# Attention and experts on one core: bias of the exponential on GpSimd, the second score half one unit later, the product with the values seven units behind

## What is computed

```python
q = (x @ Wq + bq).reshape(1, B * N, H, hd)          # x: layernorm of the input, 2048 rows
q = _fq_sym(q * scale, axis=-1)                     # s = max|q| / 127, at least 1e-8; round(q / s) * s
k = _fq_sym(k, axis=-1)
v = _fq_sym(v, axis=2)
attn = jax.nn.softmax(jnp.einsum('bhqd,bhkd->bhqk', q, k), axis=-1)
attn = _fq_unsigned(attn, axis=-1)                  # s = max / 255; round(attn / s) * s
out = jnp.einsum('bhqk,bhkd->bhqd', attn, v)
x = x + out @ Wp + bp
```

## Time and profile before

| | |
|---|---|
| median of 3 runs | 1599.62 us (1597.22 to 1603.06) |
| profiled execution | 1606.57 us, span of the trace 1604.8 us |
| TensorE, VectorE, ScalarE, GpSimd busy over the span | 83%, 65%, 53%, 53% |
| L540, 256 times | 311.9 us busy, 1218 ns each |
| L570, 256 times | 328.2 us busy, 1282 ns each |
| L493, 256 times | 536.3 us busy, 2095 ns each |
| L488, 256 times | 97.9 us busy, 382 ns each |
| L625, 256 times | 485.4 us busy, 1901 ns each |

### The profile page before, as it was taken

One profiled execution on the slowest core, in us unless ns is written; L12 is line 12 of the kernel. 1 busy time (PEld: TensorE's weight loads), 2 busy tenths in 40 slices (PEclk: granted clock), 3 DMA queues, 4 the chain that ended last, 5 costly groups with the idle time before them and its releaser, 6 DMA issues.

```text
span 1604.8 us, 28516 instructions
## 1 busy us (share of the span) xinstructions
PE 1335.0 (83%) x7922; PEld 664.3 (41%) x7923; DVE 1036.9 (65%) x1863; ACT 851.7 (53%) x1183; POOL 855.4 (53%) x772
## 2 busy tenths in 40 slices
PE   7997787778778777887877659889988998989996
PEld 3443333344344444443443334444444444444443
DVE  6456789999999999999999827623323233332331
ACT  2223699888899888898998931112211111111221
POOL 1001477677777777777776710535444444444451
PEclk9999689898898899889898969999999999999999
DMA  7332466665666556566666647276767656666455
GB/s 225 86 72 59 73 119 125 112 119 113 129 136 130 120 118 121 118 127 131 131 115 111 115 166 250 84 229 161 198 181 213 189 129 190 162 192 129 88 93 165
DMA packets 383109, 221.56 MB, mean 138 GB/s; under 512 B 344801, under 2 KB 344929, under 8 KB 378786
## 3 DMA queue, kind: packets, MB, share of 16 engines
q1 hardware_dynamic: 365186, 177.36, 45.4%
q0 software_dynamic: 17872, 43.58, 14.3%
HBM read 103.42 MB, written 36.70 MB: 87 GB/s over the span
## 4 chain that ended last, share of the span: by engine, by line
DVE 26%; PE 25%; issue 22%; DMA 19%; ACT 4%; POOL 2%; DVEq 1%; POOLq 0%; SPq 0%; ACTq 0%
DMA acc_dram<-mem 16%; DVE mem L540 15%; PE psS L750 10%; PE psS L758 4%; DVE mem L570 3%; PE psS L434 3%; PE psAV L405 2%; PE psS L1559 2%; DMA mem<-xn_dram,mem 1%; ACT mem L493 1%; PE psT L1187 1%; PE psP L1540 1%; DMA mem<-xn_dram 1%; DVE mem L516 1%; PE psP L742 1%
## 5 line engine op out<-in xcount | busy, mean ns | idle before, releaser
L625 POOL TENSOR_SCALAR mem<-mem 128x2048 bf16<-128x2048 uint8 x256 | 485.4, 1901 | 183.6 <-DMA mem<-mem 161.5
L493 ACT ACTIVATE mem<-mem 128x2048 uint8<-128x2048 f32 x256 | 536.3, 2095 | 12.4
L434 PE MATMUL psS<-mem 128*128 128x512 bf16 x1024 | 351.6, 430 | 158.4 <-DVE mem L570 114.5
L750 PE MATMUL psS<-mem 128*128 (+1 forms) x752 | 358.4, 620 | 0.0
L570 DVE TENSOR_SCALAR_CACHE_REDUCE mem<-psS,mem 128x1024 f32<-128x1024 f32 x256 | 328.2, 1282 | 23.9
L540 DVE TENSOR_SCALAR_CACHE_REDUCE mem<-psS 128x1024 f32<-128x1024 f32 x256 | 311.9, 1218 | 18.6 <-PE psS L434 18.5
L778 ACT ACTIVATE mem<-mem 128x256 f32<-128x256 f32 x94 | 39.3, 418 | 368.2 <-DVE mem L784 368.2
L1157 POOL DMA_INDIRECT acc_dram<-mem x78 | 125.4, 1607 | 195.5 <-DVE mem L1257 152.3
L784 DVE TENSOR_SCALAR mem<-psS 128x512 f32<-128x512 f32 x94 | 65.0, 692 | 220.9 <-PE psS L750 219.4
L434 PEld LDWEIGHTS psS<-mem 128*128 128x128 bf16 x1024 | 74.2, 103 | 317.2 <-DVE mem L540 146.9
L750 PEld LDWEIGHTS psS<-mem 128*128 128x128 f32 x752 | 141.6, 199 | 149.5 <-issue 147.4
(11 more groups left out here) (207 smaller groups left out, 1253.8 us busy)
## 6 DMA issues: line engine op xcount, KB each, us to landing
mem<-in_moe_w SPq DMA_DIRECT2D x33, 1536.0 KB, 9.4
mem<-in_x SPq DMA_DIRECT2D x32, 256.0 KB, 2.9
acc_dram<-mem SPq DMA_DIRECT2D x29, 256.0 KB, 2.3
mem<-mem SPq DMA_TRANSPOSE x288, 3.1
xn_dram<-mem SPq DMA_DIRECT2D x17, 256.0 KB, 2.1
mem<-in_ctx_in SPq DMA_DIRECT2D x16, 256.0 KB, 3.2
mem<-xn_dram SPq DMA_DIRECT2D x16, 256.0 KB, 4.4
mem<-acc_dram SPq DMA_DIRECT2D x16, 256.0 KB, 4.3
```

The source lines that it names most:

```text
L434: last = nc.tensor.matmul(psS[c][:, k * D:(k + 1) * D], qT[p][:, h, :], kT[:, h, c * HALF + k * D:c * HALF + (k + 1) * D], start=True, sto ...
L493: nc.scalar.activation(p8[slot], S[slot], ACT.Exp, bias=NB[:, slot:slot + 1], scale=sq[p][:, h:h + 1], accum_out=Z[p][:, h:h + 1]).then_in ...
L625: nc.gpsimd.tensor_scalar(pb[slot], pT[slot].bitcast(U8).rearrange("p (j q b) -> p j b q", b=2, q=P), 1.0, 0.0, ALU.mult, ALU.add).then_in ...
L750: last = nc.tensor.matmul(bankG[o], xT[o if xo is None else xo][:, c, :], w(c * 2 * I, 2 * I), start=(c == 0), stop=(c == DC - 1))
```

## The change

- VectorE's second half is reduced one step later: in step n it takes half 0 of unit n and half 1 of unit n-1. TensorE makes the halves in the same order.
- The bias moves from ScalarE (L488) to GpSimd, at the head of its step n. It waits for the second half of unit n there. The tile of ln 255 goes, since the value is an immediate now.
- LAG becomes 7 and BEHIND 3. The output stages stand at 9, 10, 12, 14, routing at 11 and 13, the copy of the logits at 14, the division at LAG = 7 as before, and the eviction of the transposed attention on ScalarE at h = 7.
- The query scale takes its lower bound from a tile `least` of 1e-8 instead of an immediate, as scalar_tensor_tensor; the product with QSCALE (L520) goes into the rounding instruction.
- GpSimd spreads the queries three times instead of four; the fourth part is zeroed once ahead of the loop.

```diff
-    LAG = 6
-    BEHIND = 2
-    OUT_AT = (9, 11, 13, 14)
+    LAG = 7
+    BEHIND = 3
+    OUT_AT = (9, 10, 12, 14)
...
             if there(t):
                 if h == 0:
                     pe.wait_ge(queries_moved[p], 16 * (tt + 1))
-                scores(0)
+                scores(0, n, p, h)
...
-            if there(t):
-                scores(1)
+            if within(n - 1):
+                scores(1, n - 1, p if h else 1 - p, (h - 1) % H)
...
-            if h == 10:
+            if h == 11:
                 pe_route(pe, t - 2, 0)
-            if h == 12:
+            if h == 13:
                 pe_route(pe, t - 2, 1)
...
-            if h == 8 and there(t - 1):
+            if h == 7 and there(t - 1):
                 if due(t):
                     act.wait_ge(attn_tr, t)
...
-                if h == 0:
-                    act.wait_ge(minus_ready, t + 1)
-                act.wait_ge(half_max[1], n + 1)
-                nc.scalar.activation(NB[:, slot:slot + 1], M[:, 2 * slot + 1:2 * slot + 2], ACT.Identity,
-                                         bias=ln255[:], scale=nsq[p][:, h:h + 1]).then_inc(bias_ready, 1)
                 act.wait_ge(bias_ready, n + 1)
...
-            nc.vector.tensor_scalar(sq[p], amax, QSCALE / 127.0, 1e-8, ALU.mult, ALU.max).then_inc(q_scale, 1)
+            nc.vector.scalar_tensor_tensor(sq[p], amax, QSCALE / 127.0, least, ALU.mult, ALU.max).then_inc(q_scale, 1)
             dve.wait_ge(q_scale, t + 1)
             nc.vector.reciprocal(rc, sq[p]).then_inc(q_recip, 1)
-            dve.wait_ge(q_recip, t + 1)
-            nc.vector.tensor_scalar(rz2, rc, QSCALE, None, ALU.mult).then_inc(q_factor, 1)
...
-            nc.vector.tensor_tensor(hv(q8), hv(psP[:]), bc(rz2, HD), ALU.mult).then_inc(q8_ready, 1)
+            nc.vector.scalar_tensor_tensor(hv(q8), hv(psP[:]), QSCALE, bc(rc, HD), ALU.mult, ALU.mult).then_inc(q8_ready, 1)
...
-            if h == LAG + 1 and there(t - 1):
+            if h == LAG and there(t - 1):
...
-            if there(t):
-                dve.wait_ge(scores_made[1], n + 1)
-                dve.wait_ge(half_max[0], n + 1)
-                nc.vector.tensor_scalar(S[slot][:, HALF:TK], psS[1][:], 1.0, M[:, 2 * slot:2 * slot + 1],
-                                            ALU.mult, ALU.max, accum_out=M[:, 2 * slot + 1:2 * slot + 2]).then_inc(half_max[1], 1)
-            if h == 13 and there(t - 2):
+            if within(n - 1):
+                dve.wait_ge(scores_made[1], n)
+                dve.wait_ge(half_max[0], n)
+                nc.vector.tensor_scalar(S[before][:, HALF:TK], psS[1][:], 1.0, M[:, 2 * before:2 * before + 1],
+                                            ALU.mult, ALU.max,
+                                            accum_out=M[:, 2 * before + 1:2 * before + 2]).then_inc(half_max[1], 1)
+            if h == 14 and there(t - 2):
...
-            nc.gpsimd.tensor_scalar(qst, hv(q8).unsqueeze(2).to_broadcast([P, H, 4, HD]),
+            nc.gpsimd.tensor_scalar(qst[:, :, 0:3, :], hv(q8).unsqueeze(2).to_broadcast([P, H, 3, HD]),
                                         1.0, 0.0, ALU.mult, ALU.add).then_inc(q_spread, 1)
...
+            if there(t):
+                slot = l % NS
+                if h == 0:
+                    pool.wait_ge(minus_ready, t + 1)
+                    apart(pool, t + 1)
+                pool.wait_ge(half_max[1], n + 1)
+                apart(pool, n + 1)
+                if due(n - NS + 1):
+                    pool.wait_ge(exp_done, n - NS + 1)
+                    apart(pool, n - NS + 1)
+                nc.gpsimd.tensor_scalar(NB[:, slot:slot + 1], M[:, 2 * slot + 1:2 * slot + 2],
+                                            nsq[p][:, h:h + 1], LN255, ALU.mult, ALU.add).then_inc(bias_ready, 1)
             if not isinstance(n, int) or 0 <= n - BEHIND < TT * H:
...
+            nc.gpsimd.memset(least, 1e-8).then_inc(least_ready, 1)
+            nc.gpsimd.memset(qst[:, :, 3, :], 0.0).then_inc(least_ready, 1)
```

More of the change, by code:

```diff
@@ L249, in attention_and_experts @@
         q_amax = sem("q_amax")
-        q_factor = sem("q_factor")
+        least_ready = sem("least_ready")
         q_recip = sem("q_recip")
@@ L349, in there, with within @@
             return not isinstance(t, int) or 0 <= t < TT
+        def within(n):
+            return not isinstance(n, int) or 0 <= n < TT * H
         block = es.enter_context(nc.Block())
@@ L428, in pe_step, with scores @@
             t = 2 * tt + p
-            def scores(c):
-                if due(n):
-                    pe.wait_ge(half_max[c], n)
+            def scores(c, m, pm, hm):
+                if due(m):
+                    pe.wait_ge(half_max[c], m)
                 for k in range(HALF // D):
-                    last = nc.tensor.matmul(psS[c][:, k * D:(k + 1) * D], qT[p][:, h, :],
-                                            kT[:, h, c * HALF + k * D:c * HALF + (k + 1) * D],
+                    last = nc.tensor.matmul(psS[c][:, k * D:(k + 1) * D], qT[pm][:, hm, :],
+                                            kT[:, hm, c * HALF + k * D:c * HALF + (k + 1) * D],
                                             start=True, stop=True)
@@ L534, in dve_step @@
             t = 2 * tt + p
-            slot = l % NS
+            slot, before = l % NS, (l - 1) % NS
             if there(t):
@@ L1383, in _ @@
                 nc.gpsimd.tensor_scalar(vTb[:, m, :], vT8[:, m, :], 1.0, 0.0, ALU.mult, ALU.add).then_inc(v_whole, 1)
+            pool.wait_ge(least_ready, 2)
             pool_spread(pool, 0, 0)
@@ L1507, in _ @@
                 nc.vector.tensor_scalar(vT8[:, m, :], vT[:, m, :], rv[:, m:m + 1], None, ALU.mult).then_inc(v8_ready, 1)
+            dve.wait_ge(least_ready, 1)
             dve_scale(dve, 0, 0)
```

8 lines of the change are left out of this document (2 added, 6 removed).

## The result

The changed kernel takes 1639.94 us (median of 4 runs, 1632.57 to 1646.98) against 1600.76 (1597.22 to 1603.06) for the kernel before on the same chip: 1.024 times, with a 95% interval of 1.0196 to 1.0284. It was forecast at 1592, 0.5% faster; it is 2.4% slower, and outside the range of 1567 to 1619. The profiled execution took 1641.72 us with a span of 1640.0, against a span of 1604.8 before.

The account below looks back on a forecast made before the run. VectorE, busy 95 of 100 us, was taken to bound the attention loop. A gross gain of 46.5 us less 39 us for late queries and TensorE's clock gave 7.5 us faster, 1592 on the median's scale, range 1567 to 1619.

Parts of the forecast that it names:

- The swap's gain: VectorE's two reductions per unit: 0.21 us saved in 11 of 16 units, plus 0.12, so 2.43 us a tile.
- Gross gain: VectorE in the attention loop: 16 x 2.43 from the swap plus 15 x 0.51 from the query scale, 46.5 us.
- The fourth rival: VectorE's halves: the 0.21 us does not go away, being the pipeline's end and not the semaphore; 1612 us, chance 0.09.
- The third rival: Query scale on VectorE: L516's new form does not wait for GpSimd, 10 us more gained, 1582 us; chance 0.09.
- The late queries: Tile boundary: the next tile's query transpose lands late and VectorE stalls 1.7 us at each of 15 boundaries.
- freeing it is worth nothing: ScalarE: it loses the 0.38 us of L488 but has slack already, so no gain was counted.
- All nothing: Moved eviction, output stages and routing, the values' seven-unit lag, and the memsets: no effect on the time.
- The clock: TensorE's lower granted clock: 0.25 us a tile at output matmuls, 0.65 behind the boundary wait, at 15 boundaries.
- Rival 2: TensorE's low clock lasts from the boundary into the projections, 1.7 us a tile beyond the forecast; 1618 us, chance 0.24.
- a backlog falls only 0.2 a unit: GpSimd's queue: bias and conversion take 2.15 us against VectorE's 2.36 a unit, so it fits but catches up slowly.
- The last sentence: Sign of error: if VectorE waits for exponentials rather than queries, GpSimd's backlog was sized too low.
- GpSimd 90% busy: Sign that the forecast is right: GpSimd 90% busy with little wait for DMA.

Follow-up runs that it names:

- the fastest kernel: The changed kernel with the bias back on ScalarE and the query transpose sent at h = 10 instead of 11: 1574.4 us.

## Why the prediction was wrong, point by point

**The swap's gain: right.** 1.15 us between the halves, as taken from the neighbour at h = 15. Gross gain 41.5 us measured against 46.5; of the 5 us missing, L513's longer wait is 15 x 0.16 = 2.5. The swap alone shortens VectorE's work by 37.7 us, 2.4 of them at L513, for 16 x 2.43 = 38.9. The fourth rival is out, and with it the rule of the Trainium skill as it was weighed there (VectorE: DVE Perf Modes, "The DRAIN you can't avoid"): starts moved closer by 0.21 us when the dependence on the instruction just in front went. The third rival is out too, by the 983 ns.

**The late queries: the right mechanism, sized too low.** The forecast had the issue at step 13 + 5.6, and the quoted tile has 498.55 to 504.02, 5.5. It had landing after 4.5: so it is. It had 9.1 from step 13 to step 0: 498.55 to 507.64, when L581 ends, is 9.1. It had 1.7 of stall, and the tile has 1.98, the difference being a first pair of matmuls at a lower clock (1.07 us from the first's start to VectorE's, for 0.7). Over all boundaries it is 38.9 / 15 = 2.6. The transposes are issued 5.8 us behind step 13 in the mean (5.4 to 6.1) for 5.6, because the bias of h = 11 starts at +1.7 in the mean and not at +1.3; VectorE begins 5.8 behind the issue for 5.2 (5.6 to 5.8, and 7.1 at the first boundary); and at the first and last boundary its own way is shorter. There was no stall at the boundaries before, so this costs 38.9 us more, where the forecast had 15 x 1.7 = 25.5: 13 us short.

**ScalarE and what stands in its queue: the step that failed.** The forecast has "freeing it is worth nothing" for ScalarE, and "All nothing" for the eviction and the stages that the change moves. I priced what ScalarE saved and not what stands in its queue. The copy of the next tile's input (L478) keeps its place at h = 2, and it is in no term of the sum. When the exponentials come late, so does this copy behind the one of h = 1, and TensorE's projections wait for it at h = 4. That costs 28.0 - 3.3 = 24.7 us at h = 5, and the edit that moves the copy takes that stall away. With half of the conversion left out it is 14.8 instead of 28.0, and with the halves not swapped 3.0, so it takes both the later half and the full queue of GpSimd.

**The clock: right in kind, wrong in place.** Rival 2 had the low clock last from the boundary into the projections, 1.7 us a tile more. Projections at 2.08 us for two do occur (470.18), and VectorE stands 3.43 there. But the clock was full until 468 in that tile and fell behind TensorE's wait for the copy. And it is a small share. The projections' group in the changed kernel, in the one with the copy moved, and in the kernel before:

```profile
L389 PE MATMUL psP<-mem 128*128 128x512 f32 x120 | 71.1, 677 | 0.0
```

```profile
L389 PE MATMUL psP<-mem 128*128 128x512 f32 x120 | 63.8, 613 | 0.0
```

```profile
L387 PE MATMUL psP<-mem 128*128 128x512 f32 x120 | 65.4, 628 | 0.0
```

All projections together are 5.7 us longer than before, against 24.7 us of idle at h = 5, and with the copy moved, and TensorE's wait for it gone, they are no longer than before. The 15 x 0.9 = 13.5 us that the forecast gave the clock elsewhere were 3.7 in all, if all idle time at the other heads is put down to the clock.

So the loop was missed by 33.3 us (forecast -7.5, measured +25.8): 5.0 of gain, 24.7 at h = 5, 13.4 at the head, less 9.8 that the clock did not take. The tail's 4.6 us, and the experts' 4.7, come on top; for the tail VectorE's wait before the last reciprocal grew by 2.3, and the rest was not looked into.

**GpSimd: the mis-sized term under both.** The forecast took a unit on GpSimd as 2.15 us, from durations, "a backlog falls only 0.2 a unit". Starts say 2.34, so it falls 0.02; halving the conversion took 1.0 us off each boundary and half of the stall at h = 5. The text itself says in its first part that the distance of two starts is the cost, and applied it to VectorE alone. The last sentence, that waits for exponentials would mean that GpSimd's backlog was sized too low, came true in part: VectorE waits for scores, but the scores wait for what stands behind late exponentials. The sign "GpSimd 90% busy" did not come and misled: it is 80% busy, for while TensorE and VectorE stand, its biases wait for VectorE's halves (98.3 us), and conversions stand behind them. The lateness stays in the ring without any engine being full.

**What stays open:** why the new query scale is worth twice its own time in the kernel before; the tail's 4.6 us beyond the 2.3; how the 53 us between the two kernels with the bias on GpSimd and the halves in the old order divide among the lags and the output stages.

## What to carry to other kernels

A small instruction that every unit's chain passes through should not stand in the queue of an engine that, with it, needs the whole pitch (2.34 of 2.36 us): here 0.27 us of bias on GpSimd cost 39 us, although ScalarE was the busier engine, and 9 with the halves in the old order, at a pitch of 2.57. Price an engine's unit by the distance of its starts for every engine that receives work, and compare it with the new pitch and not the old. When a pitch is shortened, list everything in each queue behind the instruction that comes later, the once-a-tile copies and DMAs too; taking one such stall away tells its cause, but only the sum of idle times tells whether it was the bound. Measure each part of a change against the kernel that has the other parts: of the fastest kernel's 25 us, 15 are the query scale's.

## What the runs showed of the hardware

- On GpSimd a one-element-per-partition instruction of 0.27 us between conversions of 1.90 costs 2.34 us a pair, start to start: 0.17 us of gaps on top of the durations.
- On VectorE a reduction that reads the accumulator result of the one just in front starts 1.36 us behind it, and 1.15 where the result is older: 0.21 us for the dependence.
- A VectorE instruction of 16 elements with two inputs in SBUF took 176 ns where no conversion ran on GpSimd, and 811 to 1446 on average beside conversions of 1.90 us; where it waited for one it ended within 0.03 us of it. With the bias on GpSimd in the kernel before, the tensor_scalar on 16 elements that copies the reciprocal took 1338 ns where it took 464:

```profile
L515 DVE TENSOR_SCALAR rz<-mem 128x16 f32<-128x16 f32 x15 | 20.1, 1338 | 0.5
```

- The granted clock fell from 1.00 to 0.50 within 2 us in which TensorE was busy 0.38 us, and stayed at 0.50 to 0.53 for the 6 us from 470, in which TensorE was busy throughout; then it was 1.00 again. These are the next stretches of the table:

```profile
472.00:474.00 2.00, 2.00 (x21) 1.12 (x20) 0.85 (x1) 1.09 (x3) 1.83 (x4) 0.50 0.82 257
474.00:476.00 2.00, 2.00 (x4) 0.68 (x4) 1.68 (x4) 2.00 (x2) 1.82 (x1) 0.53 0.70 132
476.00:478.00 2.00, 2.00 (x23) 1.07 (x21) 1.48 (x3) 1.65 (x2) 1.89 (x2) 1.00 0.30 60
```
